# Full attention: two leading part products in 32 rows for the pass that finds the maximum, heads issued in pairs

## The chip, the core and the metric

The kernel runs on one core of one Trainium2 chip. The metric is the device time of one execution in microseconds (us). The engines that matter here are TensorE (PE in the profile; its weight loads are PEld), VectorE (DVE), ScalarE (ACT), GpSimd (POOL) and SyncE (SP), which issues most DMAs. Each works through its own list in order; they meet through semaphores.

## What is computed

Eight sequences of 256 tokens go through an embedding, a first attention with relative positions, a second plain attention, a router with eight experts, and sums. The change lies in the second attention, cut to this from the reference (16 heads of 16 columns):

```
h = rmsnorm(X, norm1_w)
q = (h @ wq).reshape(B, S, N_HEADS, D_HEAD)
k = (h @ wk).reshape(B, S, N_HEADS, D_HEAD)
v = (h @ wv).reshape(B, S, N_HEADS, D_HEAD)
scores = jnp.einsum('bshd,bthd->bhst', q, k) * scale
attn = jax.nn.softmax(scores, axis=-1)
ctx = jnp.einsum('bhst,bthd->bshd', attn, v).reshape(B, S, d)
X = X + ctx @ wo
```

A softmax does not depend on what is subtracted from a row of scores, as long as the same number goes from the whole row; the row's maximum keeps the exponentials in range.

## The kernel before

**Parts.** Queries and keys are f32, but the scores are made from bf16 numbers. `project` splits each query and key into three bf16 parts (high, middle, low) and stores them to a scratch tensor in device memory, `qk_parts` (`g.qd`). The product of a query with a key is then the sum of six part products; the lists `LEFT = (0, 0, 1, 0, 2, 1)` and `RIGHT = (0, 1, 0, 2, 0, 1)` name, slot by slot, which part of the query meets which part of the key. Each slot is 16 rows (a head's 16 columns) of the tile `QK`, so the six lie under each other in 96 rows, and one matmul over 96 rows sums them. `QK` holds two sequences (`par` 0 and 1), queries and keys, and all 16 heads.

**Loads.** `load_packed` fills `QK` for one sequence with 12 DMAs of 128 KB, issued by SyncE: six slots of the queries, six of the keys. It is called twice within `project`, for sequences 0 and 1, after the stores of the first two of eight trips (L660); the stores of the later trips are issued by the same engine behind these 24 DMAs. ScalarE writes the buffer `pj_parts` that the stores read, so in trip t it first waits until the stores up to trip t - 1 have landed (`s_moved`). The other six sequences are loaded in `full_attention`, each as soon as the last part of the sequence that held its buffer has been used (`s_lg`).

**The second attention** (`full_attention`, one call, eight sequences one after the other) goes pair of heads by pair of heads. For a head, TensorE does three things:

- `scores` (L915): queries as columns 0 to 127 and 128 to 255 (two matmuls, `half`), keys as 256 moving columns, into PSUM bank 0 for even heads, bank 1 for odd ones. VectorE reduces each bank to its row maxima (L1017). This product is used for nothing but the maximum. In full it is read from all 96 rows.
- `less_max` (L928, L933): the scores again, transposed (keys in rows), and on top of them the negative maximum by a matmul with `-1` on the diagonal, into banks 2 to 5. ScalarE takes the exponential of a pair from there (L997).
- `weigh` (L943): the product with the values, for a group of four heads at a time, in four 32-column tiles of TensorE side by side. VectorE copies the sums out, twice for each sequence (`keep_out`, L1005).

**What sets the order.** TensorE's order is written out in `sequence`: `less_max` of pair hp, `scores` of the two heads of pair hp + 2, and after every second pair (hp = 2, 4, 6) the `weigh` of an earlier group. After pair 7 come the `scores` of the next sequence's first pair (`begin`), then the last `weigh`, then the `scores` of its second pair. Since there are two banks for the maximum pass, `scores` of head h waits until VectorE has reduced head h - 2 (`s_max`); VectorE reduces the heads in order.

Of the kernel before, what the change touches and what calls it, by code (L numbers as in the profile page):

```python
# [13 lines left out]
B, S, D = 8, 256, 256  # L14
T = B * S
H, DK = 16, 16
L = 32
E, F = 8, 512
P = 128
# [12 lines left out]
SLOTS = len(LEFT)  # L32
# [590 lines left out]
def project(nc, g, a):  # L623
# [8 lines left out]
    with ExitStack() as c:  # L632
# [10 lines left out]
        with nc.Block() as block:  # L643
            @block.sync
            def _(sp):
                sp.dma_start(w1[:], a["w1"]).then_inc(s_moved, 16)
                for n, w in enumerate((a["wq"], a["wk"], a["wv"])):
                    sp.dma_start(W[:, n], w).then_inc(s_moved, 16)

                def store(t):  # L650
                    for k in range(2):
                        sp.wait_ge(s_lo[k], t + 1)
                        sp.dma_start(qd[k, :, :, bass.ds(t * GC, GC)], parts[:, k].rearrange("p a (m t) -> p (a m) t", m=DC)).then_inc(s_moved, 16)


                for t in range(2):
                    store(t)
                sp.wait_ge(s_moved, 64 + 2 * 32)
                for b in range(2):
                    load_packed(g, sp, b, b)  # L660
                with sp.Fori(2, GN) as t:
                    store(t)
                sp.wait_ge(s_moved, 64 + GN * 32)
# [212 lines left out]
def load_packed(g, sp, b, par):  # L876

    src = g.qd.rearrange("k a (h d) t -> k a d h t", d=DK)
    for k, side in enumerate((LEFT, RIGHT)):
        for n in range(SLOTS):  # L880
            sp.dma_start(g.QK[n * DK:(n + 1) * DK, par, k], src[k, side[n], :, :, bass.ds(b * S, S)]).then_inc(g.s_ld[par], 16)


def full_attention(nc, g):
# [3 lines left out]
    sem, ps = g.sem, g.ps  # L888
    (s_sc, s_max, s_lg, s_exp, s_pv, s_ot, s_vs, s_pad) = (sem("fa_" + n) for n in "scores max less exp pv out values pad".split())
    s_ld, QK = g.s_ld, g.QK  # L890
    HP = H // 2
    with ExitStack() as c:
# [5 lines left out]
        with nc.Block() as block:  # L898
            @block.sync
            def _(sp):  # L900
                with sp.Fori(0, B // 2 - 1) as t:
                    for par in range(2):
                        sp.wait_ge(s_lg, (2 * t + par + 1) * HP)
                        load_packed(g, sp, 2 * t + 2 + par, par)

            @block.tensor
            def _(pe):
                mm = nc.tensor.matmul

                def scores(b, par, h):  # L910

                    if h >= 2:
                        pe.wait_ge(s_max, b * H + h - 1)
                    for half in range(2):
                        last = mm(ps[:, h % 2, half * S:(half + 1) * S], QK[:, par, 0, h, half * P:(half + 1) * P], QK[:, par, 1, h],  # L915
                                  start=True, stop=True)
                    last.then_inc(s_sc, 1)

                def less_max(b, par, hp):

                    if hp >= 2:
                        pe.wait_ge(s_exp, b * HP + hp - 1)
                    pe.wait_ge(s_max, b * H + 2 * hp + 2)
                    for k in range(2):
                        h = 2 * hp + k
                        bank = ps[:, 2 + 2 * (hp % 2) + k]
                        for jh in range(2):
                            mm(bank[:, jh * S:(jh + 1) * S], QK[:, par, 1, h, jh * P:(jh + 1) * P], QK[:, par, 0, h],  # L928
                               start=jh == 0, stop=False, skip_group_check=True)
                        for jh in range(2):  # L930
                            for half in range(2):
                                at = jh * S + half * P
                                last = mm(bank[:, at:at + P], m[:, par, h, half:half + 1].to_broadcast([P, P]), g.negIB[:],  # L933
                                          start=False, stop=True, skip_group_check=True)
                    last.then_inc(s_lg, 1)

                def weigh(b, par, grp):
                    pe.wait_ge(s_exp, b * HP + 2 * grp + 2)
                    if grp % 2 == 0:
                        pe.wait_ge(s_ot, b * 2 + grp // 2 + 1)  # L940
                    for jh in range(2):
                        for k in range(4):
                            last = mm(ps[32 * k:32 * k + PADV, 6 + grp // 2, (grp % 2) * S:(grp % 2 + 1) * S],  # L943
                                      Vs[:, par, jh, 4 * grp + k], PT[:, grp % 2, k, jh], start=jh == 0, stop=jh == 1, skip_group_check=True)
                    last.then_inc(s_pv, 1)

                def begin(b, par, loaded):
                    pe.wait_ge(s_ld[par], loaded)
                    for h in range(2):
                        scores(b, par, h)  # L950

                LOADED = 2 * SLOTS * 16

                def sequence(t, par, more):

                    b = 2 * t + par
                    for h in (2, 3):
                        scores(b, par, h)
                    pe.wait_ge(s_vs, b + 1)
                    for hp in range(HP):  # L960
                        less_max(b, par, hp)
                        for h in (2 * hp + 4, 2 * hp + 5):
                            if h < H:
                                scores(b, par, h)
                        if hp % 2 == 0 and hp:
                            weigh(b, par, hp // 2 - 1)
                    if more:
                        begin(b + 1, 1 - par, (t + 1 + par) * LOADED)
                    weigh(b, par, NG - 1)

                begin(0, 0, LOADED)
                pe.wait_ge(s_pad, 2)
                with pe.Fori(0, B // 2 - 1) as t:
                    for par in range(2):
                        sequence(t, par, True)
                sequence(B // 2 - 1, 0, True)
                sequence(B // 2 - 1, 1, False)

            @block.gpsimd
# [595 lines left out]
```

## Time and profile before

| | |
|---|---|
| median of 3 runs | 992.69 us (991.28 to 994.2) |
| the profiled execution | 995.02 us |
| its span, from first to last instruction | 993.2 us |
| mean granted TensorE clock | 0.924 of full |
| PE busy | 875.2 us (88%) |
| DVE busy | 484.8 us (49%) |
| ACT busy | 324.3 us (33%) |
| POOL busy | 152.0 us (15%) |
| second attention, first to last matmul | 438.8 to 577.7 us of the span |

Times of instructions below are from the start of the span. A granted clock of 1.00 is TensorE's 2.4 GHz, 0.50 is 1.2 GHz. Matmuls are pipelined: each lasts longer than the distance to the next one, so the start times tell the rate, and the duration tells when the result is there.

### The profile page before, as it was taken

The numbers are of one execution on the slowest core, as the hardware profiler recorded it, in microseconds if no ns is written. First come the engines' busy times: TensorE is split into PE (matmuls) and PEld (weight loads), VectorE is DVE, ScalarE is ACT, GpSimd is POOL, SyncE is SP. The second block draws the span as 40 slices with busy tenths as digits, with TensorE's granted clock in tenths as the row PEclk, the third lists the DMA queues.
The fourth block names the chain that finished last, engine by engine and source line by source line (L and its number), as shares of the span: only waits on it lengthen the run. The fifth ranks groups of instructions, "written<-read, shape, count | busy, mean of one in ns | idle before, by whom it ended". The sixth has DMA issues, their size and how long they took to land. (4 is left out here: it accounts for less than half of the span.)

```text
span 993.2 us, 20851 instructions
## 1 busy us (share of the span) xinstructions
PE 875.2 (88%) x7826; PEld 637.2 (64%) x7827; DVE 484.8 (49%) x1101; ACT 324.3 (33%) x540; POOL 152.0 (15%) x155
## 2 busy tenths in 40 slices
PE   5799899899899695969999977799989999999994
PEld 3588788788778584746666666555545555555552
DVE  7544455454445473637666758554123333333331
ACT  0454455455454142435455522220111111111110
POOL 5000000000000031420000002205602222222221
PEclk7577999989989998979999989799999999999998
DMA  6100000000000129324776320095232222222221
GB/s 220 45 2 2 2 2 2 2 2 2 2 2 2 39 77 145 96 64 66 92 98 86 42 81 0 11 372 208 103 105 39 43 43 43 43 43 43 43 37 21
DMA packets 67945, 58.72 MB, mean 59 GB/s; under 512 B 5184, under 2 KB 59528, under 8 KB 67888
## 3 DMA queue, kind: packets, MB, share of 16 engines
q1 hardware_dynamic: 60208, 47.57, 20.9%
q0 software_dynamic: 7152, 9.38, 5.7%
q8 instruction: 47, 0.77, 0.3%
q10 hardware_dynamic: 528, 0.92, 0.3%
q14 instruction: 10, 0.08, 0.0%
HBM read 34.90 MB, written 22.95 MB: 58 GB/s over the span
## 5 line engine op out<-in xcount | busy, mean ns | idle before, releaser
L408 PE MATMUL ps<-V,ErT 96*128 96x32 bf16 x2080 | 141.3, 235 | 0.0
L408 PEld LDWEIGHTS ps<-V,ErT 96*128 96x128 bf16 x2080 | 132.1, 116 | 5.4
L1017 DVE TENSOR_REDUCE fa_m<-ps 128x2 bf16<-128x512 f32 x128 | 81.8, 685 | 35.3 <-PE ps L915 34.6
L1266 POOL DMA_INDIRECT out<-ex_Y,ex_to x39 | 60.6, 1553 | 206.7 <-DVE ex_Y L1510 203.6
L547 DVE TENSOR_REDUCE la_m<-ps 128x4 bf16<-128x512 bf16 x64 | 44.3, 692 | 91.1 <-PE ps L415 91.1
L513 ACT ACTIVATE la_PT<-ps 128x512 f32<-128x512 f32 x128 | 69.4, 595 | 58.9 <-PE ps L422 58.9
L997 ACT ACTIVATE fa_PT<-ps 128x1024 f32<-128x1024 f32 x64 | 65.5, 1024 | 67.8 <-PE ps L933 67.8
L1335 PE MATMUL ps<-ex_WG,ex_xT 128*128 x156 | 78.1, 624 | 4.9 <-ACT ex_xT L1388 0.6
L1490 DVE TENSOR_TENSOR ex_hd<-ps,ex_sl 128x512 f32<-128x512 f32 x39 | 27.0, 692 | 100.5 <-PE ps L1335 100.5
L1348 PEld LDWEIGHTS ps<-ex_WD,ex_hT 128*128 128x128 f32 x312 | 59.2, 190 | 25.3 <-issue 19.3
L1348 PE MATMUL ps<-ex_WD,ex_hT 128*128 x312 | 73.8, 379 | 0.9 <-DVE ex_hT L1494 0.9
L1335 PE MATMUL ps<-ex_WU,ex_xT 128*128 x156 | 74.0, 597 | 0.0
L402 PE MATMUL ps<-XS,OH 96*128 96x256 bf16 x260 | 55.0, 296 | 12.5 <-ACT XS L486 4.5
L491 ACT ACTIVATE HS<-ps 128x512 bf16<-128x512 f32 x65 | 38.8, 597 | 75.7 <-PE ps L408 75.7
L540 DVE TENSOR_TENSOR HS<-ps,HS 128x512 bf16<-128x512 f32 x65 | 44.9, 690 | 29.6 <-PE ps L408 29.6
L1388 ACT ACTIVATE ex_xT<-ps 128x256 f32<-128x256 f32 x39 | 14.9, 383 | 126.0 <-PE ps L1328 126.0
L523 DVE CAST V<-ps 96x512 bf16<-96x512 f32 x72 | 49.0, 685 | 13.4 <-PE ps L389 9.3
L1335 PEld LDWEIGHTS ps<-ex_WU,ex_xT 128*128 128x128 f32 x156 | 30.1, 193 | 38.2 <-issue 38.2
L915 PE MATMUL ps<-QK 96*128 96x256 bf16 x256 | 44.4, 283 | 10.5 <-PEq L643 7.1
L1390 ACT ACTIVATE ex_sl<-ps 128x512 f32<-128x512 f32 x39 | 23.3, 597 | 85.4 <-PE ps L1335 85.4
L933 PE MATMUL ps<-negIB,fa_m 128*128 128x128 bf16 x512 | 50.6, 221 | 0.0
L928 PE MATMUL ps<-QK 96*128 96x256 bf16 x256 | 50.3, 278 | 0.0
(249 smaller groups left out, 1422.0 us busy)
## 6 DMA issues: line engine op xcount, KB each, us to landing
QK<-qk_parts SPq DMA_DIRECT2D x96, 128.0 KB, 5.6
qk_parts<-pj_parts SPq DMA_DIRECT2D x16, 384.0 KB, 2.8
expert_in<-SG SPq DMA_DIRECT2D x1, 5070.0 KB, 14.7
ex_XR<-expert_in SPq DMA_DIRECT2D x39, 130.0 KB, 2.0
ex_WG<-in_e_gate SPq DMA_DIRECT2D x8, 512.0 KB, 9.6
ex_WU<-in_e_up SPq DMA_DIRECT2D x8, 512.0 KB, 9.2
ex_WD<-in_e_down SPq DMA_DIRECT2D x8, 512.0 KB, 9.7
out<-HS SPq DMA_DIRECT2D x4, 512.0 KB, 3.6
```

The source lines that it names most:

```text
L402: mm(bank[:, b * H * QI:(b + 1) * H * QI], g.OH3[:, bass.ds(pair * (BP * S) + (n // NS * BP + b) * S + jh * P, P)], AQ[:, half, b, :, q0:q ...
L408: last = mm(cols[:, :, i], g.ErT[:, w0:w0 + P], q[:, :, q0 + i], start=False, stop=False, skip_group_check=True)
L513: nc.scalar.activation(PT[:, half, jh, :, k * QI:(k + 1) * QI], ps[:, 2 * (n % 2) + jh].rearrange("p (h i) -> p h i", i=QI), ACT.Exp, scal ...
L523: nc.vector.tensor_copy(QB[:, half, :, 2 * u:2 * u + 2], ps[0:KP, bank].rearrange("p (h b i) -> p b h i", h=2, b=BP)).then_inc(s_qb, 1)
L540: nc.vector.tensor_tensor(SM[:, n % 2], ps[:, 2 * (n % 2) + 1], SA[:, n % 2], ALU.max).then_inc(s_mx, 1)
L928: mm(bank[:, jh * S:(jh + 1) * S], QK[:, par, 1, h, jh * P:(jh + 1) * P], QK[:, par, 0, h], start=jh == 0, stop=False, skip_group_check=True)
L933: last = mm(bank[:, at:at + P], m[:, par, h, half:half + 1].to_broadcast([P, P]), g.negIB[:], start=False, stop=True, skip_group_check=True)
L997: nc.scalar.activation(PT[:, grp % 2, k:k + 2], ps[:, 2 + 2 * (hp % 2):4 + 2 * (hp % 2)].rearrange("p k (j i) -> p k j i", j=2), ACT.Exp, ...
L1017: nc.vector.reduce_max(m[:, par, h], ps[:, h % 2].rearrange("p (f j) -> p f j", f=2), AX.X).then_inc(s_max, 1)
L1266: nc.gpsimd.indirect_dma_start(out=outs, out_offset=bass.IndirectOffsetOnAxis(ap=to[:, n:n + 1], axis=0), in_=Y[:, n], in_offset=None, com ...
L1335: last = mm(ps[:, bk + n], xT[:, n, cc], w[:, bass.ds(e + cc * F, F)], start=cc == 0, stop=cc == 1)
L1348: last = mm(ps[:, 5, 0:D], hT[:, n, f], flatD[:, bass.ds(e + f * D, D)], start=f == 0, stop=f == FC - 1)
```

## The change

The maximum pass reads only two slots, high by high and the query's high part by the key's middle part: 32 rows in place of 96. `less_max` still sums all six, so the softmax is unchanged but for which number near the maximum is subtracted. So that the two heads of a pair can use different rows, the slots of odd heads lie in another order: slot n is put in place `n ^ 2` for n below 4, so that slots 0 and 1 are in rows 32 to 63 for odd heads, and in rows 0 to 31 for even ones. For this each load is split into one for the even and one for the odd heads, of 64 KB each. And `scores` is now called for a pair: it waits until both heads of the pair before it have been reduced, and then issues the first half of the even head, the first half of the odd one, and the second halves.

```diff
@@ load_packed
         for n in range(SLOTS):
-            sp.dma_start(g.QK[n * DK:(n + 1) * DK, par, k], src[k, side[n], :, :, bass.ds(b * S, S)]).then_inc(g.s_ld[par], 16)
+            for odd in range(2):
+                home = n ^ 2 if odd and n < 4 else n
+                sp.dma_start(g.QK[home * DK:(home + 1) * DK, par, k, odd::2], src[k, side[n], :, odd::2, bass.ds(b * S, S)]).then_inc(g.s_ld[par], 16)
@@ full_attention, TensorE
-                def scores(b, par, h):
-
-                    if h >= 2:
-                        pe.wait_ge(s_max, b * H + h - 1)
+                def scores(b, par, h0):
+
+                    if h0 >= 2:
+                        pe.wait_ge(s_max, b * H + h0)
                     for half in range(2):
-                        last = mm(ps[:, h % 2, half * S:(half + 1) * S], QK[:, par, 0, h, half * P:(half + 1) * P], QK[:, par, 1, h],
-                                  start=True, stop=True)
-                    last.then_inc(s_sc, 1)
+                        for odd in range(2):
+                            h, at = h0 + odd, slice(odd * 2 * DK, (odd + 1) * 2 * DK)
+                            last = mm(ps[:, odd, half * S:(half + 1) * S], QK[at, par, 0, h, half * P:(half + 1) * P], QK[at, par, 1, h],
+                                      start=True, stop=True)
+                            if half:
+                                last.then_inc(s_sc, 1)
@@ begin
-                    for h in range(2):
-                        scores(b, par, h)
-
-                LOADED = 2 * SLOTS * 16
+                    scores(b, par, 0)
+
+                LOADED = 2 * 2 * SLOTS * 16
@@ sequence
-                    for h in (2, 3):
-                        scores(b, par, h)
+                    scores(b, par, 2)
                     pe.wait_ge(s_vs, b + 1)
                     for hp in range(HP):
                         less_max(b, par, hp)
-                        for h in (2 * hp + 4, 2 * hp + 5):
-                            if h < H:
-                                scores(b, par, h)
+                        if 2 * hp + 4 < H:
+                            scores(b, par, 2 * hp + 4)
                         if hp % 2 == 0 and hp:
                             weigh(b, par, hp // 2 - 1)
```

What this does to the program is seen at two places. The first is TensorE's list in the attention, `scores` of heads 8 and 9 and the `weigh` behind them. Before, with the end of `less_max` ahead of it:

```order
L933 MATMUL ps<-negIB,fa_m 128x128 x4
L913 REGISTER_ALU
L915 MATMUL ps<-QK 128x256 [waits fa_max]
L915 MATMUL ps<-QK 128x256
L913 REGISTER_ALU
L915 MATMUL ps<-QK 128x256 [waits fa_max]
L915 MATMUL ps<-QK 128x256
L938 REGISTER_ALU
L940 ISA [waits fa_exp]
L943 MATMUL ps<-fa_PT,fa_Vs 32x256 [waits fa_out]
```

The same place of the changed kernel (its lines are two to five higher: L938 is the old L933, L919 the old L915, L948 the old L943):

```order
L938 MATMUL ps<-negIB,fa_m 128x128 x4
L915 REGISTER_ALU
L919 MATMUL ps<-QK 128x256 [waits fa_max]
L919 MATMUL ps<-QK 128x256 x3
L943 REGISTER_ALU
L945 ISA [waits fa_exp]
L948 MATMUL ps<-fa_PT,fa_Vs 32x256 [waits fa_out]
```

There are four matmuls as before, but one wait in place of two, ahead of all four, and it is for the maximum of the later head.

The second place is SyncE's list in `project`, where the loads of the first two sequences stand between the stores; here as a difference, with the rows around it:

```order
 L648 DMA pj_W<-in_wv 128x512
 L653 DMA qk_parts<-pj_parts 128x6x256 x4
-L881 DMA QK<-qk_parts 16x16x256 x24
+L883 DMA QK<-qk_parts 16x8x256 x48
 L661 UNCONDITIONAL_BRANCH
 L661 ISA
```

The 24 loads are now 48 of half the size; the loop behind them (L661) issues the stores of the third trip and on. In the attention each of the six later loads likewise grows from 12 to 24 DMAs.

## Rows read from the trace of the kernel before

**Rows 1.** Stretches: us, busy time (x instructions) by engine, PEclk, DMA share, GB/s

```profile
378.00:383.00 5.00, 4.88 (x23) 4.32 (x24) 2.33 (x10) 0.55 (x2) 1.53 (x2) 1.00 1.22 144
439.00:456.00 17.00, 16.51 (x164) 11.51 (x162) 11.00 (x17) 7.38 (x8) 0.88 (x2) 0.78 0.01 2
507.00:524.00 17.00, 15.88 (x196) 11.09 (x194) 11.51 (x18) 8.71 (x9) 0.00 (x0) 1.00 0.69 93
```

**Rows 2.** Groups: line, engine, operation, tiles, count | busy us, mean ns | idle before

```profile
L1017 DVE TENSOR_REDUCE fa_m<-ps 128x2 bf16<-128x512 f32 x128 | 81.8, 685 | 35.3 <-PE ps L915 34.6
L915 PE MATMUL ps<-QK 96*128 96x256 bf16 x256 | 44.4, 283 | 10.5 <-PEq L643 7.1 <-DVE fa_m L1017 1.9
```

**Rows 3.** Timeline, PE, sixth sequence: start us, us, line, matmuls merged [idle before]

```profile
512.17 0.39 PE L915 MATMUL ps<-QK 96*128 96x256 bf16 x2 [0.21 <-DVE fa_m L1017]
...
513.29 0.60 PE L915 MATMUL ps<-QK 96*128 96x256 bf16 x4
...
514.62 0.83 PE L915 MATMUL ps<-QK 96*128 96x256 bf16 x4
```

**Rows 4.** Timeline, PE, what follows on these

```profile
515.06 0.39 PE L915 MATMUL ps<-QK 96*128 96x256 bf16 x2
515.38 1.07 PE L943 MATMUL ps<-fa_PT,fa_Vs 128*32 128x256 f32 x16
516.38 0.39 PE L928 MATMUL ps<-QK 96*128 96x256 bf16 x2
...
517.28 0.60 PE L915 MATMUL ps<-QK 96*128 96x256 bf16 x4
...
519.38 0.42 PE L943 MATMUL ps<-fa_PT,fa_Vs 128*32 128x256 f32 x4
```

**Rows 5.** Timeline, DVE: the same stretch, and two pairs of the first sequence

```profile
510.83 1.28 DVE L1017 TENSOR_REDUCE fa_m<-ps 128x2 bf16<-128x512 f32 x2
...
513.71 2.62 DVE L1017 TENSOR_REDUCE fa_m<-ps 128x2 bf16<-128x512 f32 x4 [0.40 <-PE ps L915]
...
443.58 1.29 DVE L1017 TENSOR_REDUCE fa_m<-ps 128x2 bf16<-128x512 f32 x2 [1.44 <-PE ps L915]
446.14 1.29 DVE L1017 TENSOR_REDUCE fa_m<-ps 128x2 bf16<-128x512 f32 x2 [1.27 <-PE ps L915]
```

**Rows 6.** Timeline, PE, first attention: matmuls on 32 rows between others

```profile
87.13 0.55 PE L422 MATMUL ps<-negIB,la_m 128*128 128x128 bf16 x7
87.61 0.30 PE L389 MATMUL ps<-OH,tabs 32*96 32x256 bf16 x1
87.61 0.30 PE L390 MATMUL ps<-OH,tabs 32*96 32x256 bf16 x1
87.76 0.27 PE L389 MATMUL ps<-OH,tabs 32*96 32x256 bf16 x1
...
87.96 0.41 PE L444 MATMUL ps<-la_PT,HS 128*32 128x128 f32 x5
```

**Rows 7.** Timeline, PE: the last weigh of two sequences in a row

```profile
508.94 0.42 PE L943 MATMUL ps<-fa_PT,fa_Vs 128*32 128x256 f32 x4 [0.68 <-ACT fa_PT L997]
...
525.88 1.07 PE L943 MATMUL ps<-fa_PT,fa_Vs 128*32 128x256 f32 x16 [0.67 <-ACT fa_PT L997]
```

**Rows 8.** Timeline, project, and one load of the attention: SyncE and ScalarE

```profile
369.71 15.46 SPq L881 DMA_DIRECT2D QK<-qk_parts  x24
375.02 0.45 SPq L881 DMA_DIRECT2D QK<-qk_parts  x1
385.53 3.10 SPq L653 DMA_DIRECT2D qk_parts<-pj_parts  x2
395.27 1.08 ACT L755 ACTIVATE pj_parts<-ps 128x512 bf16<-128x512 f32 x2 [16.72 <-DMA qk_parts<-pj_parts]
474.18 5.76 SPq L881 DMA_DIRECT2D QK<-qk_parts  x12
```

**Rows 9.** DMA issues of the page: count, KB each, median us to landing

```profile
qk_parts<-pj_parts SPq DMA_DIRECT2D x16, 384.0 KB, 2.8
```

## Prediction

> **What bounds the kernel now.** I read the stretches first. In the second attention TensorE is busy 15.88 of 17 us at full clock, VectorE 11.51, ScalarE 8.71 [rows 1], so at first sight TensorE is the bound, and anything that shortens its work should pay. The groups say the same: the maximum pass (L915) stands idle for VectorE only 1.9 us in all, while VectorE stands idle 34.6 us for it [rows 2]. Then the timeline, for what happens between the two. Between the `weigh` at 515.38 and the next at 519.38 lie 4.00 us and two pairs of heads [rows 4], and in that time the two engines take turns at being late. Just after a `weigh` VectorE has time to spare. In the pair before the next `weigh` it has not: the odd head's `scores` start at 515.06 although the even head's started at 514.62 [rows 3, 4]; a pair's two matmuls each take 0.22, so 0.22 us are a wait. VectorE ran its four reductions there without a break, 2.62 us [rows 5]. So TensorE is the bound by a small margin: with two banks for the maximum, the loop "scores, reduce, scores" is nearly as long as TensorE's own work. At the end of a sequence a third engine sets the time: the last `weigh` waits 0.67 us for ScalarE, and from one to the next a sequence takes 525.88 - 508.94 = 16.94 us [rows 7].
>
> **The change on TensorE.** A block of `scores` is four matmuls of 256 columns before and after. What fewer rows bring is only that two can run at the same time. The trace has just that form: L389 and L390 are matmuls on 32 rows each, of 256 columns, alternating in two row groups. Both of a pair start at 87.61, the next pair at 87.76: 0.15 us for two, where L915 needs two times 0.11 [rows 6]; the 0.11 is the 0.39 of two less the 0.27 of one [rows 4]. I expect the same of the new block; it has 128 stationary columns where these have 96, so its second pair could come after 0.11 to 0.15, and I take 0.15.
>
> The same rows show what goes with it. The last of the L422 starts at 87.13 + 0.55 - 0.22 = 87.46; these follow each other at 0.055, but the first on 32 rows starts 0.15 later. So 0.09 is lost going in. Behind the last pair the next matmul starts after 0.20 where 0.11 is normal: 0.09 more going out [rows 6]. The old block cost, from the last matmul ahead of it to the first behind it, 0.055 + 4 x 0.11 = 0.49 us. The new one: 0.15 + 0.15 + 0.20 = 0.50. Between two `less_max` nothing is gained. Beside a `weigh` the old program pays the change of form already (515.06 + 0.12 to 515.38 is 0.20 [rows 4]), so there a block gets cheaper by 0.09. That is four of eight blocks a sequence, 0.37 us. The Trainium skill bears on this place: by "TensorEngine Tiling (Array Packing)", Key Properties, changing the tiling mode drains the engine; the trace agrees that a change costs, but the next matmul comes after 0.20 us and not after the 0.27 in which the last one ends. By a full drain each way a block would be 2 x 0.07 dearer, on six places of a sequence's path 0.8 us, 7 in all; I go by the rows.
>
> **The change of the wait.** `scores` of a pair now wait for both heads of the pair before. Queued behind them on TensorE are `less_max`, for which ScalarE waits, and `weigh`. The loop is then: from the start of the block to VectorE's start 0.42 before (513.29 to 513.71 [rows 3, 5]), now 0.46, since the even head's second matmul comes at 0.15 and not 0.11; two reductions 1.29 (the pairs in [rows 5]); from their end to TensorE's start 0.06 (510.83 + 1.28 = 512.11 to 512.17 [rows 3, 5]). Sum 1.81 us. TensorE's own work in that loop is the block to `less_max` 0.35, and `less_max` 0.90 + 0.09 for the way in = 0.99 (516.38 to 517.28 [rows 4]): 1.34. So where no `weigh` lies between two blocks, TensorE now stands 0.47 us. With a `weigh` (1.00 from its first matmul to `less_max` [rows 4]) it is 2.34, and VectorE's loop is covered.
>
> I walk through a sequence with this. The third pair's block starts at 512.17 as before, since its odd head waited there for the same reduction [rows 3]; before, the even one was already done. Fourth pair: 512.17 + 1.81 = 513.98 (before 513.29). Fifth: 515.79 (514.62). First `weigh`: + 0.15 + 0.20 = 516.14 against 515.38, so 0.76 late. From this `weigh` to the next: 1.00 + 0.99 + 1.81 + 0.35 = 4.15 against 4.00, 0.91 late. To the third: 1.00 + 0.99 + 0.35 + 0.99 = 3.33, which is the old length; no pair waits there. From there to the end of the sequence the chain is `less_max`, exponential, last `weigh`, none of which changes. VectorE's copies of sums (0.69 us) fall behind the pair that has a `weigh` after it, where 0.5 us and more are spare. So each sequence is 0.91 us longer. With 0.11 in place of 0.15 in the block (0.04 in each of six places) it is 0.67.
>
> The first sequence runs at a clock of 0.78 on average [rows 1], its first pairs at half of it. There a pair takes 2.56 us on TensorE [rows 5], more than the loop would, so nothing is lost in those; I put 0.4 us for it, between 0 and 0.9. The attention: 7 x 0.91 + 0.4 = 6.8 us.
>
> **The change of the loads.** In `project` 24 DMAs go out between the stores, from 369.71 for 15.46 us, and the two stores behind them at 385.53; ScalarE waits 16.72 us until 395.27 for these stores to land, and the other engines behind it [rows 8]. This wait is on the path. It is set by the bytes: at 144 GB/s [rows 1] a load of 128 KB takes 0.91 us, while its issue takes (375.02 - 369.71) / 11 = 0.48 as long as nothing holds it up [rows 8]. Now there are 48 of 64 KB: 0.455 us of transfer each, 0.48 of issue. The issue becomes the slower of the two by a little. Last issue at 369.71 + 47 x 0.48 = 392.3, over at 392.7; the stores at 393.1 and, each issued as the loads are plus its wait and register work, near 393.8, and landing 2.8 later [rows 9], or somewhat more with the first in the same queue: 396.6 to 397.3. Against 395.27 that is 1.3 to 2.0; I take 1.7. If a half load issues faster than a whole one, the bytes remain and it is 0; at 0.53 us each it would be 4.
>
> In the attention a load goes from 12 issues in 5.76 us [rows 8] to 24 in 11.5, and some 3 to land. It starts at the end of one sequence's `less_max` and is needed at the end of the next one's, about 16.5 us later: hidden, with 2 us to spare. It comes out from under cover when a half load takes 0.6 us; each 0.05 above that is 1.2 us a sequence.
>
> **Sum.** 6.8 + 1.7 = 8.5 us. The profiled execution of before took 995.02, so 1003.5 for one like it; the median of the three runs is 992.69, 2.3 less, and my forecast for the median is 992.7 + 8.5 = 1001.2.
>
> **The rivals.**
>
> *The pass gets shorter and the wait is hidden (faster).* If the reductions were done in time, only TensorE's path would count. With the switches as in [rows 6] that is 8 x 0.37 = 3.0 gained and 1.7 lost on the loads, 991.4, within what can be told. If the switches cost nothing either, each of 64 blocks saves 2 x 0.11: 14 us, less 1.7, 980.5. It decides when the loop is below 1.34 us, so the two reductions below 0.82; they take 1.29, and the wait is in the code. Half measures are likelier: a shorter loop by 0.2 us. By the Trainium skill ("TensorE: Matmul & The Clock Gate", Why this matters for your kernels) small contractions in distinct row groups run concurrently, up to 3.07 times as fast for four; taken for two it is this case. The trace agrees that they do, and not that time follows.
>
> *The two heads don't run side by side.* With 128 stationary columns, or by their banks, the four could start at 0.11 each, with the switches on top. The loop becomes 1.88, the block 0.18 longer in each of eight places. A sequence: three loops x 0.07 and five blocks x 0.18 above the 0.91, 2.0; in all 8 x 2.0 + 1.7 = 18, 1010. Against it stands what L389 and L390 do [rows 6].
>
> *The loads come late.* At 0.6 us for each half load `project` loses some 7 and the attention starts to: 1006 and up. The same kind of instruction speaks against it.
>
> *Nothing moves.* The gains at `weigh` and faster issues could cancel the loop if it is 1.6 and not 1.81: 3 lost and less, within 0.3%.
>
> **How the numbers follow.** 0.3% of 993 is 3 us, about what a measurement can tell. My case (a loss of 5 to 12) 0.70; not side by side 0.08; late loads 0.06; nothing moves 0.10; faster by over 3 us 0.06. My case's own bounds: 8 x 0.67 and loads at 0 give 998.1; 8 x 0.91 and loads at 4 give 1004. To leave out no more than 2 in 10, the range takes in half of what neither moves nor is dearer: 996 to 1009. Slower 0.84, same 0.10, faster 0.06.
>
> **What would show it.** In the changed profile: the first matmuls of two heads in one block start together, the next 0.11 to 0.15 later. VectorE is idle some 0.5 us before every pair, not in every second one only. Idle time of L919 behind the maximum grows from 1.9 us to about 0.47 x 3 a sequence, 10 or more. From last `weigh` to last `weigh` 17.8 in place of 16.94. ScalarE's long wait in `project` 18.4 in place of 16.7, with 48 issues in 23 us. I am wrong if the loop is much shorter than 1.8, if the old block's cost was not what I counted, or if TensorE's clock falls in the new idle times, which at 0.5 us between busy stretches I don't expect.

## The result, and the profile after

The changed kernel takes 1002.83 us (median of 4 runs, 1000.17 to 1005.04) against 991.99 before (median of 4, 990.82 to 994.2): a ratio of 1.0106, with an interval of 1.0074 to 1.0137. It is slower by 10.8 us. The forecast was 8.5 slower, and a median of 1001.2 in a range of 996 to 1009.

The page of the changed kernel begins so, and these are its groups for VectorE's reductions and for the maximum pass (L919 is the old L915, L1019 the old L1017):

```profile
PE 868.8 (87%) x7826; PEld 623.4 (62%) x7827; DVE 485.3 (48%) x1101; ACT 324.2 (32%) x540; POOL 152.3 (15%) x155
...
L1019 DVE TENSOR_REDUCE fa_m<-ps 128x2 bf16<-128x512 f32 x128 | 82.4, 686 | 45.2 <-PE ps L919 45.2
L919 PE MATMUL ps<-QK 32*128 32x256 bf16 x256 | 26.1, 283 | 22.8 <-DVE fa_m L1019 15.5 <-PEq L643 7.2
```

The maximum pass covers 26.1 us where it covered 44.4 [rows 2], since two of its matmuls now run at a time. What this brought is given back in the last column: it stands 15.5 us for VectorE, before 1.9, and VectorE stands 45.2 us for it, before 34.6. This is the same place of the sixth sequence as in [rows 3, 4], on TensorE (start us, us, line, merged matmuls):

```profile
535.48 0.39 PE L919 MATMUL ps<-QK 32*128 32x256 bf16 x4 [0.81 <-DVE fa_m L1019]
535.81 0.39 PE L933 MATMUL ps<-QK 96*128 96x256 bf16 x2
...
537.25 0.39 PE L919 MATMUL ps<-QK 32*128 32x256 bf16 x4 [0.38 <-DVE fa_m L1019]
...
539.03 0.39 PE L919 MATMUL ps<-QK 32*128 32x256 bf16 x4 [0.39 <-DVE fa_m L1019]
539.35 1.07 PE L948 MATMUL ps<-fa_PT,fa_Vs 128*32 128x256 f32 x16
```

and on VectorE:

```profile
535.91 1.29 DVE L1019 TENSOR_REDUCE fa_m<-ps 128x2 bf16<-128x512 f32 x2 [0.48 <-PE ps L919]
537.68 1.29 DVE L1019 TENSOR_REDUCE fa_m<-ps 128x2 bf16<-128x512 f32 x2 [0.48 <-PE ps L919]
```

The four matmuls of a block take 0.39 us from first start to last end, where they took 0.60. From block to block it is 1.77 us: 0.43 to the reductions' start, 1.29 for the two, 0.05 back. Both engines wait in every loop that has no `weigh` in it, VectorE 0.48 and TensorE 0.38 as the profile counts it; a sequence has four such waits of TensorE, the first of them (0.81) after the copy of sums. The last `weigh` of one sequence and of the next:

```profile
532.29 0.41 PE L948 MATMUL ps<-fa_PT,fa_Vs 128*32 128x256 f32 x2 [0.79 <-ACT fa_PT L999]
...
549.93 0.42 PE L948 MATMUL ps<-fa_PT,fa_Vs 128*32 128x256 f32 x4 [0.79 <-ACT fa_PT L999]
```

17.64 us, against 16.94 in [rows 7]; sequences alternate by 0.03, and the mean of seven, by ScalarE's exponentials, is 17.64 against 16.90. In `project` the loads and what waits for them (SyncE and ScalarE, as in [rows 8]):

```profile
368.71 22.62 SPq L883 DMA_DIRECT2D QK<-qk_parts  x48
392.07 1.02 SPq L653 DMA_DIRECT2D qk_parts<-pj_parts  x2
396.66 1.08 ACT L755 ACTIVATE pj_parts<-ps 128x512 bf16<-128x512 f32 x2 [19.11 <-DMA qk_parts<-pj_parts]
```

ScalarE's wait is 19.1 us in place of 16.7. By stage, from one profile of each kernel: from the first of these loads to the attention's first matmul 71.97 us against 69.05, 2.9 more; the attention, from the start of its first matmul to the start of its last, 145.24 against 138.54, 6.7 more, of which the first sequence has 1.5 and the other seven 0.74 each. That is 9.6 of the 10.0 us by which the spans differ (1003.2 to 993.2). The rest is scatter in parts that the change doesn't touch: 1.0 less ahead of the loads and 1.4 more behind the attention.

### The profile page after: what moved, and what is told of

It reads as the page before. It is cut to its first block and busy times, and to the rows that moved or that the text cites. A ratio compares the mean times of both kernels' runs of the same rounds, so it can differ in the third digit from the quotient of the medians.

```text
span 1003.2 us, 21013 instructions
## 1 busy us (share of the span) xinstructions
PE 868.8 (87%) x7826; PEld 623.4 (62%) x7827; DVE 485.3 (48%) x1101; ACT 324.2 (32%) x540; POOL 152.3 (15%) x155
## 5 line engine op out<-in xcount | busy, mean ns | idle before, releaser
L1019 DVE TENSOR_REDUCE fa_m<-ps 128x2 bf16<-128x512 f32 x128 | 82.4, 686 | 45.2 <-PE ps L919 45.2
L938 PE MATMUL ps<-negIB,fa_m 128*128 128x128 bf16 x512 | 51.1, 223 | 0.0
L933 PE MATMUL ps<-QK 96*128 96x256 bf16 x256 | 51.1, 282 | 0.0
L1337 PEld LDWEIGHTS ps<-ex_WG,ex_xT 128*128 128x128 f32 x156 | 26.9, 192 | 33.0 <-issue 33.0
```

What stands on the lines that cost most here:

```text
L1019: nc.vector.reduce_max(m[:, par, h], ps[:, h % 2].rearrange("p (f j) -> p f j", f=2), AX.X).then_inc(s_max, 1)
L1337: last = mm(ps[:, bk + n], xT[:, n, cc], w[:, bass.ds(e + cc * F, F)], start=cc == 0, stop=cc == 1)
```

## The experiments

They ran on four other chips (e1 to e4, e5 to e8, e9 to e11, and e12), where the kernel before takes 1015 to 1018 us, almost all of the difference behind the attention. The part behind it took 434.8 to 442.6 us in the twelve profiles there, whatever was changed ahead of it (415.5 and 416.9 in the first two), so whole times say less than the stages do. A profile of the unaltered kernel on one of them (e11, below) has the same times in `project` and the attention as the first one, so stages are compared across chips, and whole times only with the runs of before beside them; a difference of whole times is given by the ratio. "Sequence" is the mean time from the last exponential of one sequence to that of the next, seven in a profile.

### The loads alone

```diff
+            for odd in range(2):
+                home = n ^ 2 if odd and n < 4 else n
+                sp.dma_start(... odd heads and even heads apart ...)
-                LOADED = 2 * SLOTS * 16
+                LOADED = 2 * 2 * SLOTS * 16
```

> The loads alone: even and odd heads by separate DMAs, slots of odd heads in the other order, but TensorE's list as before (96 rows, a wait for each head). Theory (the loads cost in project only, by their issue): ScalarE's long wait in project about 19.1 us as in the changed kernel against 16.7 before, sequences in the attention 16.9 us from last weigh to last weigh as before, in all 2 to 3 us above before. Rival (the many small DMAs also disturb the attention, or the loads arrive late there): sequences longer than 16.95, in all 4 us or more above before.

1017.24 us against 1015.63 before, ratio 1.0024 (0.9999 to 1.0050): some 2 us, at the edge of what can be told. Sequence 16.89, attention 138.57 us, as before. In `project` ScalarE waited 19.7 us. So whatever the loads cost, they cost it there and nowhere else.

How much that is, one pair of profiles can't say, because the 24 whole loads themselves scatter from one profile to the next. All profiles of this study but the two with spread loads (below), sorted by the form of these loads alone:

| loads of the first two sequences | profiles | ScalarE's wait, us | first load to attention, us | first load issued to last landed, us |
|---|---|---|---|---|
| 24 of 128 KB (before, e2, e3, e5, e11, e12) | 6 | 15.6 to 18.8, mean 17.3 | 68.4 to 71.7, mean 69.9 | 22.5 to 25.8, mean 24.3 |
| 48 of 64 KB (after, e1, e4, e8, e9, e10) | 6 | 18.8 to 19.8, mean 19.5 | 71.8 to 72.4, mean 72.1 | 25.6 to 26.5, mean 26.2 |

The ranges touch, and the means differ by 2.1 us in the wait and 2.2 us in the stage. The 2.9 us of the first two profiles are on the high side.

### The pair's wait alone

```diff
-            h, at = h0 + odd, slice(odd * 2 * DK, (odd + 1) * 2 * DK)
+            h, at = h0 + odd, slice(0, KP)
```

with the loads of before.

> The pair's wait alone: the changed kernel's order and its one wait for both heads, but all 96 rows and whole loads. Theory (the wait makes the loss, the 32 rows give a part back): the loop is 0.53 + 1.29 + 0.06 = 1.88 us, a sequence 1.4 us longer than before (18.3), in all 10 to 12 us above before, 1001.5 to 1004; project as before. Rival (the change of the matmuls' form is what costs, the wait is hidden): sequences near 16.9, in all within 2 us of before.

1028.64 us, ratio 1.0122 (1.0075 to 1.0169), 12.4 us slower (expected 10 to 12). Sequence 18.32, attention 149.9 us. TensorE and VectorE in one loop of it:

```profile
517.84 0.61 PE L917 MATMUL ps<-QK 96*128 96x256 bf16 x4 [0.39 <-DVE fa_m L1017]
...
519.72 0.61 PE L917 MATMUL ps<-QK 96*128 96x256 bf16 x4 [0.38 <-DVE fa_m L1017]
...
518.38 1.29 DVE L1017 TENSOR_REDUCE fa_m<-ps 128x2 bf16<-128x512 f32 x2 [0.60 <-PE ps L917]
```

The loop is 1.88 us, to the hundredth what was expected: 0.54 + 1.29 + 0.05. The wait alone costs 1.42 us a sequence; the 32 rows side by side give 0.68 of it back, because the block they shorten now lies in the loop.

### The 32 rows alone

```diff
-QK[:, par, 0, h, half * P:(half + 1) * P], QK[:, par, 1, h],
+QK[0:2 * DK, par, 0, h, half * P:(half + 1) * P], QK[0:2 * DK, par, 1, h],
```

in the kernel before, so with its waits, and even and odd heads in the same rows (odd heads' slots 0 and 1 are there too, as loads are the old ones).

> The 32 rows alone: the maximum pass reads rows 0 to 31 for even and odd heads alike, with the waits, the order and the loads of before. No two matmuls are in different row groups. Theory (32 rows save nothing by themselves, and each block pays the change of form twice, 0.18 us, plus up to 0.04 for each second matmul): a sequence 0.3 to 0.6 us longer, 17.2 to 17.5, in all 2 to 5 us above before. Rival (fewer rows are faster by themselves): sequences below 16.9 and a time below that of before.

```profile
516.67 0.39 PE L915 MATMUL ps<-QK 32*128 32x256 bf16 x2 [0.21 <-DVE fa_m L1017]
516.99 0.39 PE L928 MATMUL ps<-QK 96*128 96x256 bf16 x2
...
517.98 0.61 PE L915 MATMUL ps<-QK 32*128 32x256 bf16 x4
```

Sequence 17.39 as expected: matmuls on 32 rows in the same row group follow each other no faster (four in 0.61 us, before 0.60), and each block pays on the way in and out. But the whole was 1.0127 (1.0075 to 1.0180), 12.9 us slower and not 2 to 5. The attention took 7.0 us more, 3.5 for seven sequences and 3.5 for the first alone. There the clock was at its lower level for longer; I come back to it. The stages of `project` and the attention account for 7.7 of the 12.9. The rest is not explained; it is no more than what the part behind the attention scatters by.

### Shorter reductions, in both kernels

```diff
-reduce_max(m[:, par, h], ps[:, h % 2].rearrange("p (f j) -> p f j", f=2), AX.X)
+reduce_max(m[:, par, h], ps[:, h % 2].rearrange("p (f j) -> p f j", f=2)[:, :, 0:P], AX.X)
```

> The changed kernel with shorter reductions: VectorE takes the maximum over half of the keys only, so this part of the result is left out. Theory (the loop through VectorE sets the time): a reduction of about 0.42 us brings the loop to about 1.25 us, below TensorE's own 1.31, and a sequence falls from 17.66 to about 15.7 us, in all 14 to 17 us below the changed kernel, near 986. Rival (the form changes and the DMAs set the time): the sequence stays above 17 and the time above 997.

> The kernel before with the same shorter reductions (the maximum over half of the keys, the rest left out), to be set beside the changed kernel with them, whose sequences took 15.77 us and whose attention took 129.8. Theory (with VectorE out of the way only TensorE's path is left, and there the new blocks are a little cheaper beside a weigh and equal elsewhere): sequences 16.1 to 16.3 us, 0.3 to 0.5 longer than those 15.77. Rival (the wait before was not VectorE's): sequences stay at 16.9.

The changed kernel with them: 1012.99 us, 0.9973 (0.9945 to 1.0001) of the kernel before beside it; the unaltered changed kernel stood at 1.0091 on another chip (e10), some 12 us above it, where 14 to 17 were expected; the attention alone is 15.4 us shorter. The kernel before with them took 1006.35 us, in one run. ScalarE's exponentials of the last pair, two sequences in a row, first in the changed kernel with short reductions, then in the kernel before with them:

```profile
505.04 1.02 ACT L999 ACTIVATE fa_PT<-ps 128x1024 f32<-128x1024 f32 x1 [0.89 <-PE ps L938]
...
520.82 1.02 ACT L999 ACTIVATE fa_PT<-ps 128x1024 f32<-128x1024 f32 x1 [0.89 <-PE ps L938]
```

```profile
503.07 1.02 ACT L997 ACTIVATE fa_PT<-ps 128x1024 f32<-128x1024 f32 x1 [0.90 <-PE ps L933]
...
519.00 1.02 ACT L997 ACTIVATE fa_PT<-ps 128x1024 f32<-128x1024 f32 x1 [0.89 <-PE ps L933]
```

15.78 and 15.93; means 15.75 and 15.90. So VectorE's reductions do set the time of the changed kernel: shortened, its sequences lose 1.9 us, those of before 1.0. The difference that is left, 0.15 us a sequence, is less than I expected (0.3 to 0.5). But the wait is not quite gone in the changed kernel with short reductions (TensorE for VectorE: us in total, times, longest):

```profile
PE ps L919 <- DVE fa_m L1019: 2.8, 8, 0.9
```

One block of each sequence still stands 0.3 us (0.9 in the first sequence) for a reduction that comes behind a copy of sums; in the kernel before with short reductions the same place costs 0.12. Without either wait the difference would be 0.15 + 0.30 - 0.12 = 0.33, within what was expected. That is an estimate; no run shows it. The whole attention took 129.8 us in the one and 129.9 in the other: the seven times 0.15 are lost again in the first sequence, 1.0 us longer, where the clock rose later.

### The loads spread over the trips

```diff
-                for b in range(2):
-                    load_packed(g, sp, b, b)
-                with sp.Fori(2, GN) as t:
+                loads = [x for b in range(2) for x in packed_parts(b, b)]
+                for t in range(2, GN):
                     store(t)
+                    share = loads[(t - 2) * len(loads) // 6:(t - 1) * len(loads) // 6]
+                    for x in share:
+                        load_part(g, sp, *x)
```

> The kernel before, with the 24 loads of the first two sequences not issued at once but four behind the stores of each of the six later trips. Theory (ScalarE's wait in project is nothing but the stores behind this queue of loads): the wait of 16.7 us goes, no wait for stores above 3 us is left, project from then to the attention is 12 to 16 us shorter and so is the whole. Rival (the bytes have to be moved on that path in any case): a gain below 5 us.

> The changed kernel with its 48 loads of the first two sequences spread in the same way, eight behind each trip's stores. Theory (the issue costs only where a queue of them stands ahead of the stores): project as long as in the spread kernel before, within 0.6 us, so that the 2.9 us that the change costs there are gone; attention 145 us as in the changed kernel. Rival (48 issues cost SyncE's time wherever they stand): project 2 us or more longer than in the spread kernel before.

In the kernel before, spread: 1005.38 us, 0.9889 (0.9852 to 0.9925) of before, 11 us faster, the fastest version of this study and ahead of both kernels. SyncE now takes turns:

```profile
374.48 2.14 SPq L653 DMA_DIRECT2D qk_parts<-pj_parts  x2
376.67 2.37 SPq L892 DMA_DIRECT2D QK<-qk_parts  x4
383.98 2.23 SPq L653 DMA_DIRECT2D qk_parts<-pj_parts  x2
```

and of ScalarE's wait for the stores 6.9 us are left, in two pieces (who waited for whom: us, times, longest):

```profile
ACT pj_parts L757 <- DMA qk_parts<-pj_parts: 6.9, 2, 4.0
```

These two are not left over from the queue: the kernel before has them too, behind its wait of 16.7 (6.7 us in two pieces, the longest 3.7). So the queue's wait is gone whole, and that a wait of 4.0 is left where none above 3 was expected says nothing against the theory. The gain in whole time is a little under the 12 to 16 expected. From the first store of the parts to the attention's first matmul it is 69.97 us, before 82.81 (82.65 in e11).

The changed kernel, spread, took 1010.38 us in one run. There the same stretch is 71.37 us, 1.4 more than in the spread kernel before; the theory had allowed 0.6, the rival had asked for 2. ScalarE's waits for stores are 6.6 us, no longer than the 6.9 above, and up to the last stores the two run alike. What differs stands behind the last stores. The last share of loads, in the spread kernel before and in the changed one:

```profile
422.09 2.60 SPq L892 DMA_DIRECT2D QK<-qk_parts  x4
```

```profile
420.55 4.11 SPq L893 DMA_DIRECT2D QK<-qk_parts  x8
425.16 0.61 PE L929 MATMUL ps<-QK 32*128 32x256 bf16 x4 [8.94 <-PEq L643]
```

All engines leave `project` together (L643). With four loads SyncE has issued them by 424.69, and the attention begins 0.45 us after the last store has landed (425.22). With eight, the last store landed at 423.24, but SyncE issues until 424.66, and the attention begins 0.50 us after that. So the wait behind the queue is gone, and 1.4 us of SyncE's issuing have come to stand on the path elsewhere. Its attention took 146.4 us, 1.1 more than in the changed kernel; two of its sequences took 18.78 us.

### The weigh in two halves

In the changed kernel, so that every loop of pairs from hp = 2 to 6 has half a `weigh` in it (those of hp = 0 and 1 stay without):

```diff
-                        if hp % 2 == 0 and hp:
-                            weigh(b, par, hp // 2 - 1)
+                        if hp >= 2 and hp < HP - 1:
+                            weigh(b, par, hp // 2 - 1, (hp % 2,))
...
+                    weigh(b, par, NG - 2, (1,))
                     weigh(b, par, NG - 1)
```

> The changed kernel with each weigh of a sequence cut in two halves (by keys), one behind the scores of each pair, so that TensorE has work in every loop of pairs and not in every second one. Theory (the 0.47 us idle in loops without a weigh is the loss): idle time of the scores behind the maximum falls from 15.5 to below 8 us, a sequence from 17.66 to 16.9 to 17.2 us, 4 to 6 us off the changed kernel, in spite of two more changes of form for each weigh. Rival (the changes of form are the loss): sequences of 17.7 us and more.

1023.90 us, 1.0105 (1.0060 to 1.0151) of before, and sequences of 17.7 us, one of 18.75: no gain, and the number is the rival's. The idle time of `scores` behind the maximum fell to 12.1 us only, not below 8, and a new one of 3.2 us stood before `less_max`. VectorE and then TensorE in the last pair:

```profile
527.88 0.69 DVE L1010 COPY OT<-ps 128x512 f32 x1 [1.32 <-PE ps L949]
528.49 1.28 DVE L1022 TENSOR_REDUCE fa_m<-ps 128x2 bf16<-128x512 f32 x2
```

```profile
529.83 0.39 PE L933 MATMUL ps<-QK 96*128 96x256 bf16 x2 [0.57 <-DVE fa_m L1022]
```

VectorE's copy stands in its list behind head 13 and waited 1.32 us for a half `weigh` that now comes a pair later; the reductions of the last pair stood behind it, and `less_max` waited for them. With the copy moved behind head 15:

```diff
-                        if h == 13:
+                        if h == 15:
                             keep_out(b, 0)
```

> The kernel with the weigh cut in two halves, and VectorE's first copy of sums moved behind the reductions of the last pair. With the halves alone that copy, in VectorE's list behind head 13, waited for a half weigh that now comes later, and held up the reductions of the last pair: less_max of pair 7 waited 0.6 us for them. Theory (that was the only new wait, the loop is otherwise covered): a sequence falls to 16.9 to 17.2 us, 4 to 6 us off the changed kernel. Rival (the two added changes of form and the loops without a weigh keep it): 17.5 us and more.

```profile
511.33 1.02 ACT L1002 ACTIVATE fa_PT<-ps 128x1024 f32<-128x1024 f32 x1 [0.46 <-PE ps L938]
...
528.39 1.02 ACT L1002 ACTIVATE fa_PT<-ps 128x1024 f32<-128x1024 f32 x1 [0.46 <-PE ps L938]
```

17.06, mean 17.03, 0.6 less than the changed kernel and within what the theory asked; 1022.67 us against 1017.87 before, 1.0029 (1.0008 to 1.0049), where the changed kernel had 1.0091 on the same chip. But most of this does not come from the place that the theory names. TensorE's waits in the attention of the changed kernel and then of this one (us in total, times, longest):

```profile
PE ps L919 <- DVE fa_m L1019: 15.5, 30, 1.4
PE ps L948 <- ACT fa_PT L999: 5.5, 7, 0.8
```

```profile
PE ps L919 <- DVE fa_m L1022: 12.5, 22, 1.4
PE ps L949 <- ACT fa_PT L1002: 2.1, 8, 0.5
```

Of the four waits for VectorE in a sequence only the last is gone, 0.39 us; the other three come ahead of the sequence's first `weigh`, where nothing was put in. The larger part, 0.57, comes from the half `weigh` that now stands before the last `weigh` and fills the wait for ScalarE there (0.79 before, 0.22 now), a wait that the kernel before has too. The rest of the sum, 0.35 the other way, is left for the added changes of form. So e8 and e9 don't show that the loops without a `weigh` were the whole loss; that rests on e2 and e4. And it still doesn't pass the kernel before.

### Both kernels again, and the clock

> The changed kernel unaltered, on the chip of the experiments, for a second profile. Sequences of 17.66 us and a wait of 19 us in project, as in the first. Of the first sequence, whose clock stood at its lower level for 13.7 us after 438.5 where before it was 10.2: if the 32 rows hold the clock down, 13.7 us or more again, and drops of the clock inside the attention can come; if it was chance, 10.2 is as likely.

> The kernel before unaltered, on the chip of the experiments, for a second profile. Sequences of 16.91 us, ScalarE's wait in project near 16.7, the clock at its lower level for 10.2 us around the attention's start and full from there to its end. What differs here from the first profile of the same kernel is the chip's and not a change's.

> The kernel with 32 rows for the maximum pass, head by head, a second time, for its clock. TensorE waits there for VectorE no longer than in the kernel before (1.9 us in all), so idle time cannot be what differs. If the 32 rows hold the clock at its lower level when the attention begins: 13.7 us or more of it again, as in all six profiles with 32 rows and whole reductions so far, against 10.2 in the five with 96 rows. If the first one's 17.1 was chance: 10.2 or less. Sequences of 17.4 us either way, but for one in which the clock falls.

e10: 1028.40 us against 1017.87, ratio 1.0091 (1.0058 to 1.0123); sequences of 17.64, but one of 18.78; ScalarE's wait 19.7; clock low for 13.7 us. e11: one run, 1020.10; sequences 16.90, wait 16.3, clock low for 10.2 us. e12: one run of 1028.45 with 1018.11 beside it; sequences 17.39, the first one again some 4 us longer than before, clock low for 17.1 us.

The granted clock is at 0.50 when the attention begins, in all profiles; TensorE has stood idle for the 7 us ahead of it. In these rows of stretches it is the third number from the end. First the kernel before:

```profile
442.00:446.00 4.00, 4.00 (x28) 3.25 (x26) 1.43 (x3) 1.31 (x2) 0.00 (x0) 0.50 0.00 0
446.00:450.00 4.00, 4.00 (x50) 2.84 (x49) 2.58 (x4) 1.83 (x3) 0.00 (x0) 0.94 0.01 2
```

The changed kernel, whose attention begins 1.9 us later:

```profile
444.00:448.00 4.00, 4.00 (x30) 2.41 (x29) 1.94 (x4) 1.48 (x2) 0.00 (x0) 0.50 0.00 0
448.00:452.00 4.00, 4.00 (x34) 2.08 (x32) 2.58 (x4) 1.59 (x2) 0.00 (x0) 0.50 0.01 2
```

The 32 rows head by head (e12), attention from 440.2:

```profile
448.00:452.00 4.00, 4.00 (x30) 2.25 (x32) 2.51 (x4) 1.49 (x2) 0.00 (x0) 0.50 0.01 2
452.00:456.00 4.00, 4.00 (x35) 2.37 (x28) 0.64 (x2) 1.02 (x1) 0.00 (x0) 0.59 0.01 4
```

From the attention's first matmul to the rise of the clock to 1.00:

| form of the maximum pass, whole reductions | profiles | us to the rise |
|---|---|---|
| 96 rows (before, e1, e2, e6, e11) | 5 | 6.7 to 8.2 |
| 32 rows, two heads side by side (after, e7, e8, e9, e10) | 5 | 9.0 to 11.4 |
| 32 rows, head by head (e3, e12) | 2 | 14.0 and 15.1 |

With the short reductions it is 4.9 with 96 rows (e5) and 8.1 with 32 (e4). The classes don't overlap. Idle time does not explain it: from the attention's start to the rise TensorE is idle 0.4 us in the kernel before and 0.4 in the head by head kernel, whose rise comes 6 to 7 us later. The pair wait on 96 rows (e2) has 1.3 us of idle time there, the paired 32 rows 1.4, and e2 rises as the others on 96 rows do. So the passes on 32 rows go with the late rise. They are not all that moves it: with the short reductions, which leave TensorE's matmuls as they are, it comes some 3 us earlier on either number of rows, in one profile each.

The clock also falls again, for 3.4 us, within the attention of e7 (twice), e8 and e10 (once each); in e10:

```profile
515.00:521.00 6.00, 4.22 (x54) 2.56 (x55) 4.29 (x8) 2.84 (x4) 0.00 (x0) 1.00 0.43 120
521.00:525.00 4.00, 4.00 (x35) 2.00 (x34) 2.55 (x4) 1.25 (x2) 0.00 (x0) 0.57 0.47 132
```

Each such fall makes its sequence 1.1 us longer (18.78 in place of 17.66). Ahead of this one TensorE was busy 4.22 of 6 us. For these falls idle time is not ruled out. They came only in kernels with the pair's wait and whole reductions, whose TensorE is idle 15 to 22 us of the attention; head by head on 32 rows it is idle 7 us, and no fall came. Of the kernels on 96 rows only e2 is idle as long (21 us), and its one profile without a fall says little, since the first profile of the changed kernel and that of e9 have none either. What in the 32 rows holds the rise back, the experiments don't tell.

## Why the prediction was right, point by point

- **The block.** Two matmuls start together and the next two after 0.12 us (taken 0.15, bounds 0.11 to 0.15); 0.15 going in and 0.20 going out, as read from L389 and L390. Right.
- **The loop.** 1.77 us against 1.81, and TensorE idle in it; e2 (1.88 with the longer block) and e4 (with reductions of 0.76 for two, a loop without a wait is 1.31, forecast 1.34 for TensorE's own work) show its terms one by one. Right, and shown: what the change does to the wait decides it, not what it does to the matmuls.
- **The sequence.** 0.74 us longer, taken 0.91, lower bound 0.67. The difference is the 0.12 for 0.15, once in each of the blocks on the path. 5.2 us in place of 6.4 for seven. The signs that were to show it are there: TensorE's idle time behind the maximum 15.5 us (forecast "10 or more"), VectorE idle 0.48 (forecast "some 0.5").
- **The first sequence.** "I put 0.4 us for it" is a term that was mis-sized: 1.5 (1.3 in e10). I took the clock's rise as fixed and only asked what its lower level hides. It comes 3 to 4 us later with the 32 rows. So the attention's total, 6.7 us against 6.8 forecast, is so close by luck: 1.2 too much for seven sequences and 1.1 too little for the first cancel.
- **TensorE's clock.** "If TensorE's clock falls in the new idle times, which ... I don't expect": not in the first profile, but in the second one of the same kernel (e10), and in two (e7, e8) of the four others with paired blocks on 32 rows. Wrong as an expectation, worth 1.1 us a time.
- **The loads in project.** Taken 1.7, measured 2.9 in the first two profiles, 2.2 as the mean of six each; e1 shows that they are the loads' alone. The issue went as forecast: 48 in 22.62 us, the stores 23.4 us behind the first load in forecast and measurement. What was mis-sized was "landing 2.8 later", with "somewhat more with the first in the same queue". From the DMA issues in that stretch of the changed kernel (count, KB each, median us to landing):

```profile
QK<-qk_parts SPq DMA_DIRECT2D x48, 64.0 KB, 3.3
qk_parts<-pj_parts SPq DMA_DIRECT2D x2, 384.0 KB, 3.7
```

  The last load landed 25.9 us after the first was issued (before: 23.6), 3.2 us after its issue had ended, so some transfers still stood in the queue when the stores came, and these landed 3.7 us after their issue in place of 2.8. That puts ScalarE's resuming 2.4 later; the remaining 0.5 of the 2.9 lies between it and the attention, and the trace shows there only that the clock was low until 404.3 us in place of 402.1. And the 16.72 and 69.05 of before, from which all this is counted, are one draw from the scatter in the table above, which a single profile could not show.
- **The queue itself.** The forecast took the wait for these stores to be set by bytes and issues standing ahead of them. e6 shows it: without the queue the wait is gone, and 12.8 us of the stretch with it.
- **The loads in the attention.** Hidden, as said; e1's sequences are those of before. Its "0.6 us" for a half load, at which they would come out from under cover, is 0.56 by its own numbers ((16.5 - 3) / 24); measured are 0.48 to 0.53 (24 in 11.50 to 12.84 us).
- **The rivals.** Side by side they ran. "Nothing moves" and "faster" fall with the loop. Whether the faster case's 3.0 us for the attention are right stays open: between e5 and e4 seven sequences gain 1.1 and the first loses 1.0, but e4 has 0.30 us of the wait left in each, e5 0.12. (Its other number, 980.5, adds up to 980.3.)
- **The rule on the drain.** By "Mode switching requires drain" in the Trainium skill ("TensorEngine Tiling (Array Packing)", Key Properties) the way out of a block would take the last matmul's 0.27 us. Measured are 0.20 to 0.21 (539.03 + 0.12 to 539.35, and 535.48 + 0.12 to 535.81), so the trace agrees with a price, not with a full drain.

## What to carry to other kernels

Before a step is made shorter, ask which loop through a second engine it lies in, and what the edit does to the point where that loop starts: two banks used one by one let VectorE and TensorE overlap, the same two banks handed over as a pair make them take turns, and here that cost 1.4 us a sequence for 0.7 gained. If heads must be issued in pairs, the other work of TensorE has to be spread over the loops that wait, and each list that waits for that work has to be read again (e8, e9); here three of the four waits lay ahead of the sequence's first `weigh` and stayed as they were, and other work for that place was not tried. And look for what stands in the longest wait of all: a queue of loads ahead of a store cost ScalarE 16.7 and 19.1 us, and spreading it was worth more than anything in the attention, though its last share must not stand behind the last store (e7). Last, before a difference of 2 or 3 us in one stage is put down to a change, look how much that stage differs among profiles in which nothing of it was changed.

## What the runs showed of the hardware

- In profiles with whole reductions TensorE's clock rose 9.0 to 11.4 us after the attention's start with the maximum pass on 32 rows side by side (five profiles) and 14.0 and 15.1 one by one (two), against 6.7 to 8.2 on 96 rows (five). TensorE was idle for 1.4, 0.4 and 0.4 to 1.3 us of that.
- The 32 row matmuls save nothing alone: four in 0.61 us. In two row groups they run in pairs 0.12 us apart at 256 columns.
- A block of them between matmuls of another form starts 0.15 us after the last of these and lets the next start 0.20 us after its own last pair, less than the 0.27 us that a matmul lasts.
- 24 loads of 128 KB in one queue took 22.5 to 25.8 us until the last had landed, 48 of 64 KB with the same 512 byte rows 25.6 to 26.5, in six profiles each; SyncE issued one in 0.47 to 0.48 us in both sizes where nothing held it up.
- The same kernel took 992 us on one chip and 1015 to 1018 on others. The attention's last matmul starts at 577.3 us in the one profile and 575.4 in the other; the difference is behind it, and I did not look for its cause.
